# Weights prepared inside the first attention, the gather ahead of the scatter, a mirrored product for the expert lists and a ring of 17 experts

## The chip, the cores and the metric

The kernel runs on one core of one Trainium2 chip. The time is device microseconds (us) of one execution; the kernel before has a median of 3058.5 us over three runs (3056.04 to 3063.08). Less is better.

## What is computed

Two layers, each an attention to a context and a feed-forward part, each added to x behind a gate `tanh(g)`. All data are float32: 4 batches of 512 rows of 512 numbers.

```
x = x + tanh(g_xattn[0]) * L0_xattn(layernorm(x), ctx, mask, wq, bq, wk, bk, wv, bv, wo, bo)   # 16 heads of 32; wq, wo in 8 bits
x = x + tanh(g_ffn[0])   * L0_ffn(layernorm(x), fp4 weights)
x = x + tanh(g_xattn[1]) * L1_xattn(layernorm(x), ctx, ...)                                      # 16 heads of 128, rotary
x = x + tanh(g_ffn[1])   * L1_ffn(layernorm(x), router_w, w_gate, w_up, w_down)

# 8-bit linear: s = max|w| / 127 per row; q = clip(round(w / s)); y = (q_x @ q_w.T) * (s_x * s_w) + b
# L1_ffn: scores = softmax(x @ router_w.T); the 8 best of 64 experts per token, their scores normalised
#         each expert takes its first 128 tokens: y = (silu(x @ w_gate[e]) * (x @ w_up[e])) @ w_down[e]
#         out[token] += y * score
```

## The kernel before

The program runs five stages, one after the other, with a barrier between them: layer0_attention, layer0_ffn, layer1_projections, layer1_attention, layer1_ffn. Each is written per engine, in blocks for SP (which issues the plain DMAs), GpSimd (POOL), ScalarE (ACT), TensorE (PE) and VectorE (DVE). Each engine follows its own list in order; semaphores tie the lists together. The change touches the first and the last stage.

**Start of the first attention.** `layer0_attention` first calls `prepare_layer0_weights` (L713), a stage of its own. There SP loads wq, wo, wk and wv (1 MB each) and five small rows (L733 to L738), and both ScalarE and VectorE wait for all nine. VectorE takes each of wq and wo through a largest value per row (L773), a scale, four scalings (L777), two rounding steps (L778, L779); TensorE transposes the rounded matrices (L758), VectorE copies them to wqT and woT (L790), wo's scales are spread over the partitions by a product with ones (L765) and copied (L794). ScalarE makes the upper halves of wk and wv for products in two parts (L748, L749), VectorE the lower ones (L797). Then come the barrier and the attention: SP loads the first context and x (L315, L318), the context is split in two parts (L415 on ScalarE, L350 on GpSimd), x is normalised and quantised. The first batch's jobs on TensorE follow JOBS_OF_FIRST: four K jobs (each 12 products, L137 to L139 in the helper mm3), four X (transposes of quantised x, L506), S (scales of x), four Q (L515; scaled by VectorE and then by ScalarE, L437), four V. Then scores (L541) of the first four heads, and the loop over groups of four heads: VectorE adds the mask and takes the maximum (shift, L657), ScalarE takes the exponential (L445), TensorE transposes the result (turn, L554), and so on.

**Routing (`route`, L1921).** For four batches of 512 rows, VectorE and TensorE normalise x, multiply it with the router's weights, and write a table of rows (x and the 64 weights of the experts) to HBM. The keys of the chosen tokens are put in keyT, 128 partitions: partition e holds expert e in the first half of the tokens, partition 64 + e the same expert in the second. VectorE takes the 128 largest of each partition by 16 rounds of max and match_replace (L2160, L2161). TensorE then moves the second half's lists to partitions 0 to 63 (L2071); 16 more rounds over both lists (L2168, L2169) give each expert's first 128 tokens; three more steps fill empty slots with the numbers of spare rows, TensorE transposes (L2073), and VectorE writes `slots` (L2177). During routing SP loads the weights of the first 13 experts (L2361, L2362): two at first, then three after each of the four stores of the table; behind them go 17 stores of zeros to second_sum (L1990).

**Experts (`experts`, L2187).** For each of 64 experts: GpSimd gathers 128 rows of the table (L2223), TensorE transposes them (turn_x, L2278), gate and up products (L2288), TensorE transposes h (L2296), down product (L2305), VectorE scales it by the router's weight (L2333), GpSimd scatters it with addition to `out` or, for odd experts, to second_sum (L2232). TensorE's order in iteration e is gate_up(e), turn_h(e - 1), turn_x(e + 1), down(e - 1). Four buffers (AHEAD) hold gathered rows, so that the gather of e + 4 waits for the scaling of e. In GpSimd's list it stands behind the scatter of e. A ring of 13 places (RING_E) holds the experts' weights; SP loads expert e once the down product of e - 13 is done. At the end second_sum is added to `out` by four DMAs (L2239).

Of the kernel before, what the change touches and what calls it, by code (L numbers as in the profile page):

```python
# [178 lines left out]
def make_constants(pool, c, made):  # L179
# [17 lines left out]
JOBS_OF_FIRST = [("K", 0), ("K", 1), ("K", 2), ("K", 3), ("X", 0), ("X", 1), ("X", 2), ("X", 3), ("S", 0),  # L197
                 ("Q", 0), ("Q", 1), ("Q", 2), ("Q", 3), ("V", 0), ("V", 1), ("V", 2), ("V", 3)]
# [45 lines left out]
def layer0_attention(nc, d, x_out):  # L244

    with ExitStack() as ctx:
# [15 lines left out]
        prepare_layer0_weights(nc, d, c, gate, wqT, woT, swq, bqs, bk, swo_row, bv_row, bo_row, wk, wv, bank)  # L262

# [28 lines left out]
        turn_ps, o_ps = bank[4:6], bank[6]  # L292
        names = ("c_loaded c_hi c_lo mhalf_made stat_ready rstd_ready normed x_scaled diagonal x_round x_quant job_done free_act free_dve "
                 "sx_out q_raw q_made scored shifted expd turned ev_act ev_dve weighed oT_out backed o_part o_scaled o_round "
                 "o_quant gbo_made x_biased y_made added step_dve")
# [12 lines left out]
        with nc.Block() as block:  # L308

            @block.sync  # L310
            def _(sp):
                def load(b):
                    if b:
                        sp.wait_ge(s["c_lo"], KC * b)
                    sp.dma_start(ctx_f[:], ctxT_src[b]).then_inc(s["c_loaded"], 16)  # L315
                    if b >= 3:
                        sp.wait_ge(stored[b % 3], 16 * NT)
                    sp.dma_start(x4[:, b % 3], x_src[b]).then_inc(x_loaded[b % 3], 16)  # L318

# [7 lines left out]
                load(0)  # L327
                load_mask(0)
                load_mask(1)
                load(1)  # L330
                for t in range(TILES):
                    sp.wait_ge(s["shifted"], H0 * (t + 1))
                    if t + 2 < TILES:
                        load_mask(t + 2)
                    if t % NT == NT - 1 and t // NT + 2 < B:
                        load(t // NT + 2)
                    if t:
                        store(t - 1)
# [5 lines left out]
            def _(pool):  # L344
                pool.memset(mhalf4[:], -0.5).then_inc(s["mhalf_made"], 1)

# [40 lines left out]
                pool.tensor_scalar(bo_row[:], bo_row[:], gate[:], 1.0, ALU.mult, ALU.mult).then_inc(s["gbo_made"], 1)  # L387
                pool.wait_ge(s["gbo_made"], 1)
                context_lo(0)
                normalise(0)  # L390
                quantise_x(0)
                for G in range(GROUPS0 + DRAIN0):
# [16 lines left out]
            def _(act):  # L409
# [53 lines left out]
                context_hi(0)  # L463
                for job in JOBS_OF_FIRST:
                    evict((job[0], 0, job[1]))
                    make_q((job[0], 0, job[1]))
# [19 lines left out]
            def _(pe):  # L486
                def do(job):
# [5 lines left out]
                    if kind in "KV":  # L493
                        if i == 0:
                            pe.wait_ge(s["c_lo"], KC * b + KC)
                        for a in range(KC):
# [13 lines left out]
                    elif kind == "Q":  # L510
                        if i == 0:
                            by, nth = rank[("X", b, 3)]
                            pe.wait_ge(free[by], nth)
                        for a in range(KC):
# [64 lines left out]

                for job in JOBS_OF_FIRST:  # L580
                    do((job[0], 0, job[1]))
                scores(0)
                for G in range(GROUPS0 + DRAIN0):
# [13 lines left out]
            def _(dve):  # L597
# [92 lines left out]

                dve.wait_ge(s["mhalf_made"], 1)
                statistics(0, 0, NT)
                scale_x(0, 0, NT)
                for job in JOBS_OF_FIRST:
                    evict((job[0], 0, job[1]))
                for G in range(GROUPS0 + DRAIN0):
                    g, b = G % 16, G // 16
                    for i in range(4):
                        shift(4 * G + i)
# [12 lines left out]

def prepare_layer0_weights(nc, d, c, gate, wqT, woT, swq, bqs, bk, swo_row, bv_row, bo_row, wk, wv, bank):  # L713

    with ExitStack() as ctx:
        st = Stage(nc, ctx, "w0")
        sb, sem = st.sb, st.sem
        nat = [sb(f"nat{i}", [P, KC, D], F32) for i in range(2)]
        full = [sb(f"full{i}", [P, KC, D], F32) for i in range(2)]
        q_int = [sb(f"q_int{i}", [P, KC, D], BF16) for i in range(2)]  # L720
        tmp = sb("tmp", [P, KC, D], F32)
        bq = sb("bq", [P, KC], F32)
        amax, scale, inv = (sb(n, [P, 2, KC], F32) for n in ("amax", "scale", "inv"))
        diag = sb("diag", [P, KC, P], F32)
        loaded, made, rounded, turned, copied, spread, spread_out, split_hi, split_lo, step_dve, gated = (
            sem(n) for n in "loaded made rounded turned copied spread spread_out split_hi split_lo step_dve gated".split())
        LOADS = 9
        with nc.Block() as block:

            @block.sync  # L730
            def _(sp):
                for to, of in ((nat[0], "L0_wq"), (nat[1], "L0_wo"), (full[0], "L0_wkT"), (full[1], "L0_wvT")):
                    sp.dma_start(to[:], d[of].rearrange("(k p) n -> p k n", p=P)).then_inc(loaded, 16)  # L733
                sp.dma_start(bq[:], d["L0_bq"].rearrange("(p k) -> p k", p=P)).then_inc(loaded, 16)
                sp.dma_start(bk[:], d["L0_bk"].rearrange("(p k) -> p k", p=P)).then_inc(loaded, 16)
                sp.dma_start(bv_row[:], row_of(d["L0_bv"], 0, D)).then_inc(loaded, 16)
                sp.dma_start(bo_row[:], row_of(d["L0_bo"], 0, D)).then_inc(loaded, 16)
                sp.dma_start(gate[:], row_of(d["g_xattn"], 0, 1)).then_inc(loaded, 16)  # L738

            @block.gpsimd  # L740
            def _(pool):
                make_constants(pool, c, made)

            @block.scalar
            def _(act):
                act.wait_ge(loaded, 16 * LOADS)
                act.activation(gate[:], gate[:], ACT.Tanh).then_inc(gated, 1)
                act.activation(wk[0][:], full[0][:], ACT.Copy).then_inc(split_hi, 1)  # L748
                act.activation(wv[0][:], full[1][:], ACT.Copy).then_inc(split_hi, 1)  # L749

            @block.tensor
            def _(pe):
                pe.wait_ge(made, CONSTS)
                for w in range(2):
                    pe.wait_ge(rounded, w + 1)
                    for j in range(KC):
                        for k in range(KC):
                            mm = pe.transpose(bank[w * KC + j][:, :].bitcast(BF16)[:, k * P:k * P + P],  # L758
                                              q_int[w][:, j, k * P:k * P + P], c["identb"][:])
                        mm.then_inc(turned, 1)  # L760
                pe.wait_ge(spread, 1)

                pe.wait_ge(copied, 1)
                for j in range(KC):
                    mm = pe.matmul(bank[0][:, j * P:j * P + P], c["ones"][:], diag[:, j], start=True, stop=True)  # L765
                mm.then_inc(spread_out, 1)

            @block.vector
            def _(dve):
                step = Chain(dve, step_dve)  # L770
                dve.wait_ge(loaded, 16 * LOADS)
                for w in range(2):
                    step(dve.tensor_reduce(amax[:, w], nat[w][:], AX.X, ALU.max, apply_absolute_value=True))  # L773
                    step(dve.tensor_scalar(scale[:, w], amax[:, w], float(np.float32(1 / 127)), 1e-8, ALU.mult, ALU.max))
                    step(dve.reciprocal(inv[:, w], scale[:, w]))
                    for j in range(KC):
                        step(dve.tensor_scalar(tmp[:, j], nat[w][:, j], inv[:, w, j:j + 1], 127.0, ALU.mult, ALU.min))  # L777
                    step(dve.tensor_scalar(tmp[:], tmp[:], -127.0, ROUND, ALU.max, ALU.add))  # L778
                    dve.tensor_scalar(q_int[w][:], tmp[:], ROUND, None, ALU.subtract).then_inc(rounded, 1)  # L779

                dve.tensor_scalar(swq[:], scale[:, 0], SCALE0, None, ALU.mult)
                dve.tensor_scalar(bqs[:], bq[:], SCALE0, None, ALU.mult)
                dve.wait_ge(made, CONSTS)
                for j in range(KC):
                    ds = dve.tensor_scalar(diag[:, j], c["ident"][:], scale[:, 1, j:j + 1], None, ALU.mult)
                ds.then_inc(spread, 1)
                for w, to in enumerate((wqT, woT)):
                    for j in range(KC):
                        dve.wait_ge(turned, w * KC + j + 1)
                        dve.tensor_copy(to[:, :, j * P:j * P + P],  # L790
# [1389 lines left out]
F1 = 192  # L2180
FP = F1 // 2
AHEAD = 4
RING_E = 13
PARTS = 4


# [245 lines left out]
```

## Time and profile before

| | |
|---|---|
| median of three runs | 3058.5 us |
| the profiled execution | 3060.83 us |
| its span | 3059.0 us |
| TensorE busy | 2639.5 us (86%) |
| VectorE busy | 1738.9 us (57%) |
| ScalarE busy | 1272.6 us (42%) |
| GpSimd busy | 805.6 us (26%) |
| granted TensorE clock, mean | 0.943 |

Times in the rows are from the start of the span. Busy time excludes the issuing of DMAs and waiting. A granted clock of 1.00 is full speed. The first attention runs until about 480 us, the routing from 2498 to 2626 us, the experts from there to 3031 us, and the last addition to the end.

### The profile page before, as it was taken

How to read it: one execution, taken by the hardware profiler on the slowest of the kernel's cores; microseconds unless marked ns; L12 is line 12 of the kernel's file. 1: busy time of each engine (PE TensorE's matmuls, PEld its weight loads, DVE VectorE, ACT ScalarE, POOL GpSimd, SP SyncE). 2: the span in 40 equal slices, each digit the busy share in tenths (PEclk: the TensorE clock that was granted, in tenths of full speed). 3: DMA queues.
4: the chain of work that ended last, by engine and by line, in shares of the span. 5: the costliest groups of instructions: out<-in, count | busy, mean ns of one | idle time of the engine just before them, and what ended most of it. 6: DMA issues, size and time to landing. Idle time of an engine off the chain costs nothing. (4 is left out here: it accounts for less than half of the span.)

```text
span 3059.0 us, 48349 instructions
## 1 busy us (share of the span) xinstructions
PE 2639.5 (86%) x17099; PEld 2107.4 (69%) x17099; DVE 1738.9 (57%) x3888; ACT 1272.6 (42%) x3385; POOL 805.6 (26%) x825
## 2 busy tenths in 40 slices
PE   3888988579999599999699999999999972588885
PEld 2555655479999488887588888888888862345452
DVE  4767676674433566666466666666666647422221
ACT  1666666222222344444355555555555531121111
POOL 2222311000000255555222222222222210244443
PEclk8999998789999799999799999999999986799998
DMA  3010100330000555555712421421331138499986
GB/s 124 12 46 19 46 19 19 111 95 15 29 28 8 173 182 187 192 186 186 222 50 56 134 54 43 124 67 40 91 109 42 36 102 291 127 290 290 272 219 113
DMA packets 227055, 340.10 MB, mean 111 GB/s; under 512 B 24512, under 2 KB 110976, under 8 KB 226304
## 3 DMA queue, kind: packets, MB, share of 16 engines
q1 hardware_dynamic: 211904, 297.14, 31.3%
q0 software_dynamic: 14912, 39.85, 5.8%
q8 instruction: 139, 2.28, 0.3%
q14 instruction: 100, 0.82, 0.1%
HBM read 230.60 MB, written 110.53 MB: 112 GB/s over the span
## 5 line engine op out<-in xcount | busy, mean ns | idle before, releaser
L1706 POOL TENSOR_SCALAR a_prob<-a_prob,a_rinv 128x640 f32<-128x640 f32 (+3 forms) x256 | 252.4, 986 | 770.2 <-DVE a_rinv L1861 770.2
L1851 DVE TENSOR_REDUCE a_mx<-a_s_ps 128x1 f32<-128x640 f32 (+3 forms) x256 | 262.3, 1025 | 274.2 <-PE a_s_ps L1775 267.9
L1727 ACT ACTIVATE a_probT<-a_t_ps 128x512 fp32r<-128x512 f32 (+3 forms) x512 | 237.2, 515 | 369.4 <-PE a_t_ps L1783 369.4
L1867 DVE TENSOR_TENSOR a_probT<-a_t_ps,a_probT 128x512 fp32r<-128x512 f32 (+3 forms) x512 | 276.7, 582 | 47.2 <-ACT a_probT L1727 47.1
L1718 ACT ACTIVATE a_prob<-a_s_ps,a_nb,a_rs 128x640 f32<-128x640 f32 (+3 forms) x256 | 267.7, 1046 | 0.0
L137 PE MATMUL a_o_ps<-a_probT,a_v 128*128 128x256 f32 x832 | 245.4, 295 | 0.0
L139 PE MATMUL a_o_ps<-a_probT,a_v 128*128 128x256 f32 x832 | 235.1, 283 | 0.0
L138 PE MATMUL a_o_ps<-a_probT,a_v 128*128 128x256 f32 x832 | 235.1, 283 | 0.0
L1783 PE MATMUL a_t_ps<-a_ident,a_prob 128*128 128x128 f32 x1664 | 225.9, 274 | 8.5 <-DVE a_probT L1867 5.9
L137 PE MATMUL f_bank<-f_xT,f_gu 128*128 128x256 f32 x704 | 204.9, 291 | 19.1 <-DVE f_gu L1114 19.1
L554 PE MATMUL a_bank<-a_ident,a_prob 128*128 128x128 f32 x1024 | 168.2, 291 | 58.9 <-ACT a_prob L445 33.8
L554 PEld LDWEIGHTS a_bank<-a_ident,a_prob 128*128 128x128 f32 x1024 | 113.4, 144 | 152.7 <-ACT a_prob L445 112.8
L1783 PEld LDWEIGHTS a_t_ps<-a_ident,a_prob 128*128 128x128 f32 x1664 | 194.4, 141 | 31.3 <-issue 6.1
L138 PE MATMUL f_bank<-f_xT,f_gu 128*128 128x256 f32 x704 | 203.6, 289 | 0.0
L139 PE MATMUL f_bank<-f_xT,f_gu 128*128 128x256 f32 x704 | 203.5, 289 | 0.0
L445 ACT ACTIVATE a_prob<-a_prob,a_nmax 128x512 f32<-128x512 f32 x256 | 182.1, 716 | 18.6 <-DVE a_nmax L657 18.6
L2325 DVE SCALAR_TENSOR_TENSOR e_h<-e_th,e_gu_ps 128x192 f32<-128x192 f32 x64 | 22.7, 355 | 282.1 <-ACT e_th L2266 282.1
L2288 PE MATMUL e_gu_ps<-m_wgu,e_xT 128*128 128x384 f32 x512 | 180.0, 495 | 1.4 <-ACT e_xT L2249 1.4
L137 PE MATMUL p_bank<-p_w,p_xT 128*128 128x512 f32 x384 | 159.6, 416 | 17.0 <-DVE p_w L1475 11.8
L657 DVE CUSTOM_DVE_ANT_0 a_prob<-a_bank,a_mask 128x512 f32<-128x512 f32 x256 | 161.5, 687 | 18.4 <-PE a_bank L541 13.4
L138 PEld LDWEIGHTS a_o_ps<-a_probT,a_v 128*128 128x128 f32 x832 | 158.5, 190 | 5.6
L137 PEld LDWEIGHTS a_o_ps<-a_probT,a_v 128*128 128x128 f32 x832 | 158.3, 190 | 5.5
(299 smaller groups left out, 6737.9 us busy)
## 6 DMA issues: line engine op xcount, KB each, us to landing
m_wgu<-in_w_gate SPq DMA_DIRECT2D x64, 384.0 KB, 3.9
m_wgu<-in_w_up SPq DMA_DIRECT2D x64, 384.0 KB, 5.4
m_wd<-in_w_down SPq DMA_DIRECT2D x64, 384.0 KB, 7.6
l_q_hi<-p_turned SPq DMA_DIRECT2D x64, 256.0 KB, 2.7
l_q_lo<-p_turned SPq DMA_DIRECT2D x64, 256.0 KB, 2.5
a_qT<-l_q_hi SPq DMA_DIRECT2D x64, 256.0 KB, 3.6
a_qT<-l_q_lo SPq DMA_DIRECT2D x64, 256.0 KB, 4.2
l_v_hi<-p_vs SPq DMA_DIRECT2D x32, 256.0 KB, 2.7
```

Of the source, the lines that this page charges most:

```text
L137: pe.matmul(out, ll, rh, start=first, stop=False, **kw)
L138: pe.matmul(out, lh, rl, start=False, stop=False, **kw)
L139: return pe.matmul(out, lh, rh, start=False, stop=last, **kw)
L445: act.activation(prob[:, n % RING0], prob[:, n % RING0], ACT.Exp, bias=nmax[:, n % RING0:n % RING0 + 1], scale=-1.0, accum_out=rsum[:, T % ...
L554: mm = pe.transpose(turn_ps[n % 2][:, a * P:a * P + P], prob[:, n % RING0, a * P:a * P + P], c["ident"][:])
L1706: pool.tensor_scalar(prob[:, k % 4, 0:w], prob[:, k % 4, 0:w], rinv[:, k % 4:k % 4 + 1], 1.0, ALU.mult, ALU.mult).then_inc(s["weighted"], 1)
L1718: act.activation(prob[:, k % 4, 0:w], s_ps[:, k % 2, 0:w], ACT.Exp, bias=nb[:, k % 4:k % 4 + 1], scale=rs[:, u, h:h + 1], accum_out=rsum[: ...
L1727: act.activation(probT[0][:, pair % 2, i * 4:i * 4 + n, k % 2], t_ps[i][:, 0:n * P].rearrange("p (m n) -> p m n", n=P), ACT.Copy).then_inc ...
L1783: mm = pe.transpose(t_ps[i][:, m * P:m * P + P], prob[:, k % 4, (i * 4 + m) * P:(i * 4 + m + 1) * P], c["ident"][:])
L1851: step(dve.tensor_reduce(mx[:, k % 4:k % 4 + 1], s_ps[:, k % 2, 0:w], AX.X, ALU.max))
L1867: dve.tensor_tensor(probT[1][:, pair % 2, i * 4:i * 4 + n, k % 2], t_ps[i][:, 0:n * P].rearrange("p (m n) -> p m n", n=P), probT[0][:, pai ...
L2288: mm = pe.matmul(gu_ps[e % 2][:, 0:2 * F1], xT[:, e % 2, k], wgu[:, u, :, k], start=(k == 0), stop=(k == KC - 1))
```

## The change

1. `prepare_layer0_weights` is gone. The same steps are put into the lists of `layer0_attention`, in buffers that its first batch does not use yet. SP loads the context first, then wk, x, wv, wq, wo. The V jobs move ahead of the X jobs. VectorE quantises wq before the V evictions and finishes wo after the first four shifts; TensorE waits for wo before its first turn.
2. The second 16 rounds of the lists are gone. The list of 128 partitions is transposed at once; a product with a mirrored identity turns the second half's list upside down, so that it fills the first half's empty slots from the back. Four VectorE steps write `slots`. The last match_replace of the first rounds is left out.
3. The ring has 17 places. Routing's x, table and transposed x lie in the last six of them; their loads (experts 11 to 16) go behind the stores of zeros and a wait for the table's stores.
4. In the experts, GpSimd issues the gather of e + 4 before the scatter of e.

The core of the diff:

```diff
-JOBS_OF_FIRST = [("K", 0), ("K", 1), ("K", 2), ("K", 3), ("X", 0), ("X", 1), ("X", 2), ("X", 3), ("S", 0),
-                 ("Q", 0), ("Q", 1), ("Q", 2), ("Q", 3), ("V", 0), ("V", 1), ("V", 2), ("V", 3)]
+JOBS_OF_FIRST = [("K", 0), ("K", 1), ("K", 2), ("K", 3), ("V", 0), ("V", 1), ("V", 2), ("V", 3),
+                 ("X", 0), ("X", 1), ("X", 2), ("X", 3), ("S", 0), ("Q", 0), ("Q", 1), ("Q", 2), ("Q", 3)]
...
@@ SP
+                load_context(0)
+                sp.dma_start(k_full, rows(d["L0_wkT"])).then_inc(s["wk_loaded"], 16)
+                sp.dma_start(bk[:], columns("L0_bk")).then_inc(s["wk_loaded"], 16)
+                load_x(0)
+                sp.dma_start(v_full, rows(d["L0_wvT"])).then_inc(s["wv_loaded"], 16)
...
+                sp.dma_start(natural[0], rows(d["L0_wq"])).then_inc(s["wq_loaded"], 16)
...
+                sp.dma_start(natural[1], rows(d["L0_wo"])).then_inc(s["wo_loaded"], 16)
...
@@ ACT
                 context_hi(0)
+                act.wait_ge(s["wk_loaded"], 32)
+                act.activation(wk[0][:], k_full, ACT.Copy).then_inc(s["kw_hi"], 1)
+                act.wait_ge(s["wv_loaded"], 32)
+                act.activation(wv[0][:], v_full, ACT.Copy).then_inc(s["vw_hi"], 1)
...
@@ PE
+                pe.wait_ge(s["consts_made"], CONSTS)
                 for job in JOBS_OF_FIRST:
+                    if job == ("X", 0):
+                        turn_weights(0)
                     do((job[0], 0, job[1]))
                 scores(0)
+                turn_weights(1)
+                spread_scales()
+                pe.wait_ge(s["w_copied"], 2 * KC + 1)
@@ DVE
+                dve.wait_ge(s["kw_hi"], 1)
+                dve.tensor_tensor(wk[1][:], k_full, wk[0][:].bitcast(F32), ALU.subtract).then_inc(s["kw_lo"], 1)
                 dve.wait_ge(s["mhalf_made"], 1)
                 statistics(0, 0, NT)
+                dve.wait_ge(s["vw_hi"], 1)
+                dve.tensor_tensor(wv[1][:], v_full, wv[0][:].bitcast(F32), ALU.subtract).then_inc(s["vw_lo"], 1)
                 scale_x(0, 0, NT)
-                for job in JOBS_OF_FIRST:
+                dve.wait_ge(s["wq_loaded"], 32)
+                largest(0)
+                step(dve.tensor_scalar(swq[:], wscale[:, 0], SCALE0, None, ALU.mult))
+                step(dve.tensor_scalar(bqs[:], bq[:], SCALE0, None, ALU.mult))
+                scale_weights(0)
+                round_weights(0)
+                for i in range(2):
+                    evict(("V", 0, i))
+                dve.wait_ge(s["wo_loaded"], 48)
+                largest(1)
+                for i in range(2, 4):
+                    evict(("V", 0, i))
+                copy_weights(0, wqT)
+                scale_weights(1)
+                for job in JOBS_OF_FIRST[8:]:
                     evict((job[0], 0, job[1]))
+                for i in range(4):
+                    shift(i)
+                round_weights(1)
...
+                ds.then_inc(s["spread"], 1)
+                copy_weights(1, woT)
+                dve.wait_ge(s["spread_out"], 1)
+                dve.tensor_copy(swo_row[:], bank[4][:]).then_inc(s["w_copied"], 1)
...
@@ route
                 for j in range(B):
                     store_tab(j)
-                    prefetch(2 + 3 * j, min(5 + 3 * j, RING_E))
+                    prefetch(2 + 3 * j, min(5 + 3 * j, RING_E - SHARED_E))
                 for g in range(OUT_ROWS // P):
                     sp.dma_start(second[g * P:g * P + P], zeros[:, 0:D]).then_inc(s["zero_stored"], 16)
+                sp.wait_ge(s["logits_done"], B * NT)
                 for u in range(2):
                     sp.wait_ge(stored[u], 16 * (B // 2))
+                prefetch(RING_E - SHARED_E, RING_E)
...
-                pe.matmul(slot_ps[0:E, 0:CAP], c["ident"][:, E:2 * E], lists[:, 0], start=True, stop=True).then_inc(s["moved"], 1)
-                pe.wait_ge(s["firsts_ready"], 1)
-                pe.transpose(slot_ps[:, CAP:CAP + E], first[:], c["ident"][0:E, 0:E]).then_inc(s["slots_turned"], 1)
+                pe.transpose(slot_ps[:, 0:P], lists[:], c["ident"][:]).then_inc(s["lists_turned"], 1)
+                pe.wait_ge(s["turned_copied"], 1)
+                pe.matmul(slot_ps[:, P:P + E], mirror[:], turned[:, 1], start=True, stop=True).then_inc(s["mirrored"], 1)
...
-                both = lists[0:E].rearrange("e l n -> e (l n)")
-                for r in range(CAP // TOP):
-                    best8 = first[:, r * TOP:r * TOP + TOP]
-                    step(dve.max(best8, both))
-                    step(dve.match_replace(both, best8, both, 0.0))
...
+                step(dve.scalar_tensor_tensor(chosen[:], turned[:, 0], 0.0, slot_ps[:, P:P + E], ALU.is_equal, ALU.mult))
+                step(dve.tensor_tensor(chosen[:], chosen[:], turned[:, 0], ALU.add))
+                step(dve.tensor_scalar(spare[:], chosen[:], 0.0, slot_no[:], ALU.is_equal, ALU.mult))
+                dve.scalar_tensor_tensor(slots[:, 0:E], spare[:], float(T), chosen[:], ALU.add, ALU.subtract).then_inc(s["slots_ready"], 1)
...
@@ experts
                     pool.wait_ge(s["scaled"], e + 1)
+                    gather(e + AHEAD)
                     if e >= 2:
                         pool.wait_ge(scattered[e % 2], 16 * (e // 2))
                     pool.indirect_dma_start((out, second)[e % 2][:], bass.IndirectOffsetOnAxis(ap=slots[:, e:e + 1], axis=0), yw[:, e % AHEAD], None,
                                             bounds_check=OUT_ROWS - 1, compute_op=ALU.add).then_inc(scattered[e % 2], 16)
-                    gather(e + AHEAD)
...
-RING_E = 13
+RING_E = 17
+SHARED_E = 6
```

## Rows read from the trace of the kernel before

**Rows 1.** Timeline, first 55 us: start us, us, engine, line, what.

```profile
16.16 2.29 DVE L773 TENSOR_REDUCE w_amax<-w_nat 128x4 f32<-128x2048 f32 x1 [16.16 <-DMA a_gate<-in_g_xattn]
...
29.47 1.23 DVE L779 TENSOR_SCALAR w_q_int<-w_tmp 128x2048 bf16<-128x2048 f32 x1
...
32.44 2.02 PE L765 MATMUL a_bank<-w_diag,a_ones 128*128 128x128 f32 x8
32.86 1.42 DVE L790 COPY a_woT<-a_bank 128x512 bf16<-128x512 bf16 x4
...
35.10 2.28 DVE L797 TENSOR_TENSOR a_wk<-w_full,a_wk 128x2048 fp32r<-128x2048 f32 x1
...
40.26 0.38 SPq L315 DMA_DIRECT2D a_ctx_f<-in_ctxT  x1
...
51.49 0.80 PE L137 MATMUL a_bank<-a_ctx_s,a_wk 128*128 128x512 f32 x1 [17.03 <-POOL a_ctx_s L350]
```

**Rows 2.** DMA issues, 0 to 80 us: count, KB, us to landing (issue at 2.33).

```profile
w_full<-in_L_wvT SPq DMA_DIRECT2D x1, 1024.0 KB, 11.8
```

**Rows 3.** Timeline, 64 to 87 us.

```profile
64.38 1.33 PE L506 MATMUL a_bank<-a_identb,a_qx 128*128 128x128 bf16 x16
...
69.20 3.50 ACT L437 ACTIVATE a_q<-a_qraw,a_bqs,a_swq 128x512 f32<-128x512 f32 x4 [1.99 <-DVEq L638]
...
70.62 0.58 PE L137 MATMUL a_bank<-a_wv,a_ctx_s 128*128 128x512 f32 x1
...
82.77 1.14 PE L541 MATMUL a_bank<-a_k,a_q 32*128 32x512 f32 x8 [0.88 <-DVE a_v L640]
...
85.62 1.37 PE L554 MATMUL a_bank<-a_ident,a_prob 128*128 128x128 f32 x8 [1.72 <-ACT a_prob L445]
...
85.86 0.69 DVE L657 CUSTOM_DVE_ANT_0 a_prob<-a_bank,a_mask 128x512 f32<-128x512 f32 x1
```

**Rows 4.** Timeline, end of the routing.

```profile
2606.27 1.21 DVE L2161 MATCH_REPLACE8 r_keyT<-r_lists,r_keyT 128x1024 f32<-128x1024 f32 x1
2607.59 0.69 PE L2071 MATMUL r_slot_ps<-r_lists,r_ident 128*64 128x128 f32 x2 [42.24 <-DVEq L2162]
...
2625.67 0.22 DVE L2177 CAST m_slots<-r_slot_ps 128x64 uint32<-128x64 f32 x1 [0.46 <-PE r_slot_ps L2073]
```

**Rows 5.** Timeline of SP in the routing: the stores of zeros.

```profile
2574.53 15.43 SPq L1990 DMA_DIRECT2D second_sum<-r_zeros  x17
```

**Rows 6.** Chain of waits in the experts: start us, us, what.

```profile
2709.09 0.75 PE e_x_ps L2278 x4
2709.84 1.73 PE e_y_ps L2305 x4
...
2711.59 0.76 DVE e_yw L2333
...
2713.15 1.25 POOL second_sum L2232
...
2715.04 6.30 DMA e_xg<-token_table,m_slots
...
2794.23 2.90 PE e_y_ps L2305 x4
```

**Rows 7.** The scalings as one group, 2646 to 2958; chain, last experts.

```profile
L2333 DVE TENSOR_SCALAR e_yw<-e_y_ps,e_xg x51: 749/751/752, 2646.3 to 2953.9; 128x512 f32<-128x512 f32 x51
...
3000.53 2.58 PE e_gu_ps L2288 x8
3005.78 2.58 PE e_gu_ps L2288 x8
```

**Rows 8.** Stretches: us, busy PE, PEld, DVE, ACT, POOL, PEclk, DMA share, GB/s.

```profile
2788.00:2798.00 10.00, 7.75 (x23) 4.33 (x22) 2.21 (x4) 1.20 (x3) 2.64 (x2) 0.83 0.80 230
2646.30:2957.40 311.10, 273.99 (x910) 155.99 (x909) 73.71 (x151) 60.25 (x151) 133.79 (x102) 0.97 0.98 281
```

**Rows 9.** Timeline of TensorE within 2788 to 2798.

```profile
2793.10 1.13 PE L2278 MATMUL e_x_ps<-e_ident,e_xg 128*128 128x128 f32 x4 [2.25 <-DMA e_xg<-token_table,m_slots]
```

More of the change, by code:

```diff
@@ L311, in _, with load_context @@
             def _(sp):
-                def load(b):
+                def load_context(b):
                     if b:
@@ L335, in _ @@
                     if t % NT == NT - 1 and t // NT + 2 < B:
-                        load(t // NT + 2)
+                        load_context(t // NT + 2)
+                        load_x(t // NT + 2)
                     if t:
@@ L689, in scale_out, with largest, scale_weights @@
                         dve.reciprocal(oinv[:, u:u + 1], os[:, u:u + 1]).then_inc(s["o_scaled"], 1)
+                def largest(w):
+                    step(dve.tensor_reduce(wmax[:, w], natural[w], AX.X, ALU.max, apply_absolute_value=True))
+                    step(dve.tensor_scalar(wscale[:, w], wmax[:, w], float(np.float32(1 / 127)), 1e-8, ALU.mult, ALU.max))
+                    step(dve.reciprocal(winv[:, w], wscale[:, w]))
+                def scale_weights(w):
+                    for j in range(KC):
+                        step(dve.tensor_scalar(scaled_w[:, j], natural[w][:, j], winv[:, w, j:j + 1], 127.0, ALU.mult, ALU.min))
@@ new lines, in round_weights, with copy_weights @@
+                def round_weights(w):
+                    step(dve.tensor_scalar(scaled_w, scaled_w, -127.0, ROUND, ALU.max, ALU.add))
+                    if w:
+                        dve.wait_ge(s["w_turned"], KC)
+                    dve.tensor_scalar(q_int, scaled_w, ROUND, None, ALU.subtract).then_inc(s["w_rounded"], 1)
+                    dve.wait_ge(s["w_rounded"], w + 1)
+                def copy_weights(w, to):
+                    for j in range(KC):
+                        dve.wait_ge(s["w_turned"], w * KC + j + 1)
+                        dve.tensor_copy(to[:, :, j * P:j * P + P],
+                                        bank[4 + j][:, :].bitcast(BF16)[:, 0:D].rearrange("p (k n) -> p k n", k=KC)
+                                        ).then_inc(s["w_copied"], 1)
@@ L696, in _ @@
+                dve.wait_ge(s["spread_out"], 1)
+                dve.tensor_copy(swo_row[:], bank[4][:]).then_inc(s["w_copied"], 1)
+                dve.wait_ge(s["gated"], 1)
                 for G in range(GROUPS0 + DRAIN0):
                     g, b = G % 16, G // 16
-                    for i in range(4):
+                    for i in range(4 if G else 0):
                         shift(4 * G + i)
@@ L709, in _ @@
                             scale_x(b + 1, 2 * (g - 3), 2 * (g - 3) + 2)
-        st.clear()
[L713 to L790, printed above, removed]
-                                        bank[w * KC + j][:, :].bitcast(BF16)[:, 0:D].rearrange("p (k n) -> p k n", k=KC)
-                                        ).then_inc(copied, 1)
-                dve.wait_ge(spread_out, 1)
-                dve.tensor_copy(swo_row[:], bank[0][:])
-                for i, w in enumerate((wk, wv)):
-                    dve.wait_ge(split_hi, i + 1)
-                    dve.tensor_tensor(w[1][:], full[i][:], w[0][:].bitcast(F32), ALU.subtract).then_inc(split_lo, 1)
@@ L1918, with route @@
 HALF = T // 2
-def route(nc, d, x_in, table, out, slots, load, second):
+def route(nc, d, x_in, table, out, slots, ring, load, second):
     with ExitStack() as ctx:
@@ L1946, in route @@
         keyT = sb("keyT", [P, HALF], F32)
-        lists = sb("lists", [P, 2, CAP], F32)
-        first = sb("first", [E, CAP], F32)
-        empty = keyT[0:E, 0:CAP]
+        lists = sb("lists", [P, CAP], F32)
+        turned = sb("turned", [P, 2, E], F32)
+        chosen, spare = sb("chosen", [P, E], F32), sb("spare", [P, E], F32)
         x_ps = [ps(f"x_ps{i}", [P, D], F32) for i in range(NT)]
@@ L2362, in load @@
             eng.dma_start(wd[:, u], d_src[e]).then_inc(w_loaded[u], 16)
-        route(nc, d, x_in, table, out, slots, load, second)
+        route(nc, d, x_in, table, out, slots, ring, load, second)
         experts(nc, table, out, second, slots, wgu, wd, w_loaded, load)
```

102 lines of the change are left out of this document (76 added, 26 removed).

## Prediction

> **What bounds the kernel now.** I read the busy slices first, then the stretches that the change touches (the start, the routing, the experts) instruction by instruction, then the chain of waits. At the start VectorE sets the pace: it prepares the weights from 16.2 us on, and only when all is ready does the attention ask for its context (40.26) and start its first product (51.49); the first attention weights are turned at 85.62 [rows 1, 3]. Between the two attentions nothing is edited. In the routing VectorE alone makes the lists: a last round ends at 2607.5, the merging of two lists per expert ends with the slot numbers at 2625.9 [rows 4]. In the experts TensorE is busy for 274 of 311 us, and the DMA engines 0.98 of the time [rows 8]. Two readings of that stretch are possible. The chain of waits repeats this loop, two experts long: the gather lands, its rows are turned (0.75), the down product of two experts before (1.73) ends, VectorE scales it (0.76), GpSimd issues the scatter (1.56 from the scale's start), and the next gather only 1.89 later; that one lands 6.30 after its start [rows 6]. The sum is 0.75 + 1.75 + 1.56 + 1.89 + 6.30 + 0.05 = 12.3 us for two experts, 6.15 each, and the count agrees: 51 scalings, the first at 2646.3, the last at 2953.9, are 50 steps of 6.15 us [rows 7]. The other reading is that the transfers fill the DMA engines. 311.1 us at 281 GB/s are 87.4 MB, 1.72 MB per expert; that the rate stays at 281 could be the cause of the 6.15 or its result. Without loads TensorE goes on at 5.25 us per expert (3000.53 to 3005.78) [rows 7].
>
> **Part 1, weights prepared inside the attention.** The old chain to 40.26 goes; its pieces come back beside the first products. Landing: the fourth megabyte landed at 2.33 + 11.8 = 14.1 us [rows 2], about 2.65 us each after a first at some 6.2, so context 6.2, wk 8.9, x 11.5, wv 14.5, wq 17.2, wo 20 with its small rows 21.5. The context's split took until 11.2 us after its issue (40.26 to 51.49), so it is ready at 12.0. ScalarE's copy of wk (taken as long as VectorE's subtraction of it, 2.28) ends at 11.2, the subtraction at 13.5: products begin at 13.6. K takes 12.9 (51.49 to 64.38), to 26.5; V, now next, about 11.1 (from 70.62 to some 1.0 before 82.77), to 37.6 [rows 1, 3]. In that time VectorE does statistics and scaling of x and quantises wq; the old chain needed (30.7 - 16.16)/2 = 7.3 us per matrix [rows 1], x some 9 from its landing (an estimate: eight steps of about 0.7 [rows 3] and GpSimd's between them), so wq is ready near 30.5 and V's products hide it (7 us to spare). On the path again: 16 transposes of wq and their copies, 1.9 us (an estimate: the copies alone are 1.42), to 39.5; then X, S and Q to the last q, 8.3 (64.38 to 72.70), to 47.8; scores and four shifts, 3.8 (82.77 to 86.55), to 51.6 [rows 1, 3]. Then wo: two rounding steps of 1.23, to 54.1; the diagonal (estimated at 0.9) beside the transposes, copies 1.42, to 56.4; the scales spread 2.0 and copied 0.7 (as long as a shift), to 59.1 [rows 1, 3]. TensorE waits for all this before turn(0), which now stands at 85.62: **26.5 us less**. Bounds: ScalarE, VectorE and GpSimd wait in new places (ScalarE's wv copy is ahead of its K evictions; VectorE's V evictions stand behind the quantising of wq and the largest of wo). If wo's last steps (7.5 us) hid wholly behind other work the gain would be 34; if wq's quantising ended 7 us later than I have it and then some, 20. I take 26.5, as both were followed step by step.
>
> **Part 2, lists.** From the end of the last round to the slot numbers are now 2625.89 - 2607.48 = 18.4 us [rows 4]. The last match (1.21 + 0.09) goes too. New: a turn of 128x128 on TensorE (two half products took 0.69, with 0.1 ahead), a copy (0.3), the mirrored product (0.4 to 0.7), four steps on 128x64, nearest to the final cast's 0.22, with 0.05 between: 0.8 + 0.3 + 0.6 + 1.1 = 2.8, say 3.0; ends 2 and 4.5. That makes 1.3 + 18.4 - 3.0 = **16.7 us**. VectorE was the only engine at work there, so all of it counts, if SP is done by then.
>
> **Part 3, the ring.** Loads 11 to 16 are issued behind the 17 zero stores and a wait for the tables. SP needed 15.43 us for those 17, 0.91 each [rows 5]: it is held by the filled queue. Starting between 2569 (six load issues of before are out of the way) and 2574.5, with 18 issues at 0.91 to 1.36 (by size, 384 to 256 KB), SP ends between 2601 and 2614; slots are ready at 2609.2. So cost 0 to 5, taken 0. In the experts four loads fewer remain (47 for 51), 4.7 MB. With gathers as the bound that is worth nothing.
>
> **Part 4, gather ahead of scatter.** The 1.89 us leave the loop: 12.3 - 1.9 = 10.4 us for two experts, 5.2 each, and TensorE's own 5.25 takes over. The gather no longer has its expert's scatter just ahead in GpSimd's queue. The scatter comes 1.4 us later; behind it on GpSimd is only the next wait for a scaling, and it has two experts (10.5 us) to land. With no slack, gathers that land late still cost: I put 0.15 us per expert, 5.40: 50 x (6.15 - 5.40) = **38 us** (ends: 5.25 gives 45; 5.96, see A, 12). The clock is part of this: after TensorE had waited 2.25 us for a gather, its four transposes took 1.13 for 0.75 and the down product after them 2.90 for 1.73, 1.6 us more, and the granted clock of 2788 to 2798 is 0.83 where the whole stretch has 0.97: for a part of these 10 us it was at the lower of its levels, 1.2 GHz [rows 6, 8, 9].
>
> A row first: gathers took 6.30 us while loads kept the DMA engines at 0.98 [rows 6, 8]. The Trainium skill (DMA: Bandwidth & Descriptors, "Queues, rings and completion order") says that each DMA engine takes turns between its queues, a packet at a time. By that rule a longer line of loads in SP's queue would not lengthen a gather in GpSimd's, and the experts would reach 5.25, 45 us; no run here shows it under a longer line.
>
> **Sum.** 26.5 + 16.7 + 38 = 81.2. The profiled span is 3059.0 us, its time 3060.8 (1.8 outside the span), 2.3 above the median of the three runs, 3058.5. 3060.8 - 81.2 - 2.3 = 2977.3: **2977 us**.
>
> **Rivals.** (A) The DMA engines are the bound. For it: share 0.98 [rows 8]. With the missing 0.02 used, and 1% more, 1.72 MB need 5.96 us. Against: the chain runs through gathers, never through a load [rows 6], and a line of loads can grow by 0.7 us per expert for 47 experts, 33 us, before it uses up the ring's 17 x 5.25 = 89. It holds only if gathers are stretched with the loads. Then 46 steps of 5.96 and four of 5.25 take 295 us for 307.6: 26.5 + 16.7 + 12.4 = 55.6, **3003 us**. (B) The start and SP's late loads cost more: wq not hidden (20 for 26.5) and SP 3.5 us late, together 10: **2987 us**. (C) Slower: behind the longer line of loads gathers land so late that TensorE idles 2.2 us and the clock falls each time. One turn of two experts is then 10.5 + 2.2 + 1.6 = 14.3, 7.15 each, which loses 50 us against the 43 of parts 1 and 2. That begins at gathers of 10.5 + 2.2 - 4.1 = 8.6 us, where 6.30 is the row; against it speaks that the DMA engines are full already while it takes 6.30. At 9.5 us a turn is 15.2, 7.6 each, and the time 3058.5 - 43.2 + 72.5 = **3088 us**. (D) The new order does not do what it says: the gather, started 1.9 us earlier, takes 1.9 us longer, as it now competes with more of the loads. Then only parts 1 and 2 stay, **3015 us**.
>
> **How the numbers follow.** Forecast (5.25 to 5.6 us per expert) 0.62; A 0.18; B 0.10; D 0.07; C 0.03. The forecast's own range is 2962 to 2992 (experts -7 and +10, start -8 and +7, not all at once). The range for 8 in 10 takes A and B in and leaves C, most of D and a double gain out: **2957 to 3010**. About 0.2%, 6 us, is what can be told from no change. All but C are faster by more; C starts about at no change: faster 0.97, within 0.01, slower 0.02.
>
> **What would show it.** In the changed kernel: first K product near 13.6 and first transposed attention weights near 59 us; slot numbers some 3 us after the last maximum; SP's last ring load issued before them; gather issue 0.8 us after each scaling's end, scatter behind it; TensorE's idle time before the transposes of gathered rows down to a quarter; steps of scaling 5.25 to 5.5. The forecast falls if gathers take over 6.7 us from issue to landing, if TensorE begins to wait for ring loads, or if the first turn stands beyond 65 us.

## The result and the profile after

The changed kernel takes 3009.2 us (median of four runs, 3002.4 to 3010.7) against 3057.3 before: a ratio of 0.984, 95% interval 0.982 to 0.986, 48 us less where 81 were forecast. The kernel before has a median of 3057.3 us here, and of 3062.0 and 3060.3 beside the two sets of experiments below; kernels of different sets can be compared to some 5 us only. The profiled execution has a span of 3006.6 us for 3059.0, and these 52.4 us can be placed by where each stage begins in the two traces:

| stretch | before | after | less | forecast |
|---|---|---|---|---|
| start of the span to the first DMA of the routing | 2498.1 | 2471.7 | 26.4 | 26.5 |
| routing, to the first gather | 130.4 | 117.4 | 13.0 | 16.7 |
| first gather to last scatter | 397.3 | 384.4 | 13.0 | 38 |
| last scatter to the end | 33.2 | 33.2 | 0 | 0 |

So the experts gave 25 us less than forecast and the routing 4. The start first, in the timeline of the changed kernel (start us, us, engine, line, what):

```profile
14.23 0.77 PE L137 MATMUL a_bank<-a_ctx_s,a_wk 128*128 128x512 f32 x1 [14.23 <-DVE a_wk L777]
...
49.38 2.09 PE L580 MATMUL a_bank<-a_k,a_q 32*128 32x512 f32 x8 [3.74 <-ACT a_q L465]
...
56.60 1.89 PE L625 MATMUL a_bank<-a_identb,a_probT 128*128 128x128 bf16 x16 [5.13 <-DVE a_probT L766]
...
59.10 2.04 PE L633 MATMUL a_bank<-a_diag,a_ones 128*128 128x128 f32 x8 [0.61 <-DVE a_woT L772]
61.18 0.69 DVE L808 COPY a_swo_row<-a_bank 128x512 f32<-128x512 f32 x1 [2.23 <-PE a_bank L633]
61.93 1.97 PE L593 MATMUL a_bank<-a_ident,a_prob 128*128 128x128 f32 x8 [0.79 <-DVE a_swo_row L808]
```

The first product stands at 14.2 where it stood at 51.49 [rows 1], and turn(0) at 61.93 where it stood at 85.62 [rows 3]. That is 23.7 us, and it is what the edit gives where it ends. The other 2.7 do not come from it. Followed through the two traces, the lead falls to 19.7 us by 473 us of the kernel before (copies of L666, now L728) and rises to 26.8 by the end of the first attention, which lasts until 564 us and not 480. The same instructions took 74.0 us before and 66.9 after there, beside another granted clock (us, busy PE, PEld, DVE, ACT, POOL, granted clock, DMA share, GB/s; first before, then after):

```profile
473.00:547.00 74.00, 61.19 (x647) 37.12 (x647) 52.02 (x148) 46.91 (x124) 11.45 (x12) 0.88 0.05 16
```

```profile
453.30:520.20 66.90, 53.96 (x645) 33.58 (x647) 51.90 (x148) 46.85 (x124) 11.48 (x12) 1.00 0.05 17
```

Seven kernels here have the new start. In their traces turn(0) stands at 61.0 to 62.0 us, but the routing begins anywhere from 2466.1 to 2473.7, where the three kernels with the old start have 2495.8 to 2498.4. So 22 to 32 us of lead reach the routing, though the edit gives nearly the same each time.

The lists in the routing, same view:

```profile
2582.50 1.23 DVE L2196 MAX8 r_lists<-r_keyT 128x8 f32<-128x1024 f32 x1
...
2583.93 0.45 PE L2107 MATMUL r_slot_ps<-r_ident,r_lists 128*128 128x128 f32 x1 [41.02 <-DVEq L2199]
2584.42 0.29 DVE L2202 COPY r_turned<-r_slot_ps 128x128 f32<-128x128 f32 x1 [0.45 <-PE r_slot_ps L2107]
...
2584.77 0.69 PE L2109 MATMUL r_slot_ps<-r_turned,r_mirror 128*128 128x64 f32 x2 [0.38 <-DVE r_turned L2202]
...
2586.37 0.23 DVE L2209 SCALAR_TENSOR_TENSOR m_slots<-r_spare,r_chosen 128x64 uint32<-128x64 f32 x1
```

From the last maximum (2583.73) to the slots (2586.60) are 2.9 us, where 18.4 followed the last replacement of before [rows 4].

In the experts the chain of waits still runs through the gather (start us, us, what):

```profile
2702.74 1.73 PE e_y_ps L2339 x4
...
2704.49 0.76 DVE e_yw L2367
...
2706.02 7.68 DMA e_xg<-token_table,m_slots
...
2713.74 0.75 PE e_x_ps L2312 x4
2714.49 1.73 PE e_y_ps L2339 x4
...
2717.77 8.12 DMA e_xg<-token_table,m_slots
```

The scatter is gone from the loop: the gather starts 1.53 us after the scaling's start and not 3.45 [rows 6]. But it takes 7.7 to 8.1 us and not 6.3. A turn of two experts is 0.75 + 1.75 + 1.53 + 7.7 = 11.7 to 12.2 us for 12.3. GpSimd's rows show the two steps of a turn: 5.25, then mostly 6.2 to 7.3. TensorE is busy for 175 us of the 200 from 2660 to 2860, for 177 in the kernel before. From the second to the 51st scatter the mean step is 5.95 for 6.17, in the last twelve before the last it is 5.14 for 5.64.

### The profile page after: what moved, and what is told of

The parts are those of the page before. It is cut to its first block and busy times, and to the rows that moved or that the text cites. A ratio compares the mean times of both kernels' runs of the same rounds, so it can differ in the third digit from the quotient of the medians.

```text
span 3006.6 us, 48204 instructions
## 1 busy us (share of the span) xinstructions
PE 2631.6 (88%) x17077; PEld 2105.2 (70%) x17099; DVE 1724.5 (57%) x3837; ACT 1274.4 (42%) x3385; POOL 809.0 (27%) x827
## 5 line engine op out<-in xcount | busy, mean ns | idle before, releaser
L2322 PE MATMUL e_gu_ps<-m_ring,e_xT 128*128 128x384 f32 x512 | 179.2, 493 | 1.4 <-ACT e_xT L2283 1.4
L719 DVE CUSTOM_DVE_ANT_0 a_prob<-a_bank,a_mask 128x512 f32<-128x512 f32 x256 | 161.4, 687 | 19.3 <-PE a_bank L580 14.3
L1416 ACT ACTIVATE p_sq<-p_bank 128x128 f32<-128x128 f32 x384 | 101.1, 278 | 146.6 <-PE p_bank L139 146.6
L138 PEld LDWEIGHTS a_o_ps<-a_probT,a_v 128*128 128x128 f32 x832 | 158.4, 190 | 5.6
```

The costliest lines, as they stand in the source:

```text
L138: pe.matmul(out, lh, rl, start=False, stop=False, **kw)
L2322: mm = pe.matmul(gu_ps[e % 2][:, 0:2 * F1], xT[:, e % 2, k], wgu[:, u, :, k], start=(k == 0), stop=(k == KC - 1))
```

## The experiments

Two theories for the step of 5.95. Theory 1 is rival A: the transfers fill the DMA engines, and bytes by rate set the step. Theory 2: the loop through the gather sets it, and the gather has become longer. The first four kernels were to tell them apart, and to find out what the ring and the lists do by themselves.

### The old order in the changed kernel

```diff
                     pool.wait_ge(s["scaled"], e + 1)
-                    gather(e + AHEAD)
...
                     pool.indirect_dma_start((out, second)[e % 2][:], ...)
+                    gather(e + AHEAD)
```

> The changed kernel with the old order on GpSimd: scatter of e, then gather of e + 4. Theory 1 (the DMA engines are full with 285 GB/s and set the step of about 5.95 us per expert, whichever goes first): gathers take 6.3 us again instead of 7.8, the step stays within 0.05 us of 5.95, the whole within 3 us of the changed kernel's 3009. Theory 2 (the loop through the gather sets the step and the gather was stretched only because its place moved): the loop gets its 1.9 us back and the gather stays near 7.8, step 6.15 or more, 10 us or more slower than 3009.

Measured: 3018.6 us, 0.987 of before (0.984 to 0.990) where the changed kernel has 0.984 (0.982 to 0.986); by the traces the stretch from first gather to last scatter is 390.6 us for 384.4. The medians of the two sets, 3018.6 and 3009.2, differ by 9.4 us, or by 4.7 when each is taken from the kernel before run beside it, and the intervals of the ratios overlap. Over all the traces with four buffers and all loads, that stretch is 390.1 to 397.3 us with the scatter first (four kernels, the kernel before and two with its expert code among them) and 380.5 and 384.4 with the gather first. So the order is worth something between 6 and 17 us. The step is 6.03 for 5.95, just outside what theory 1 allowed and below the 6.15 of theory 2. The gather's length settles part of it. The view by tile of the gathered rows, 2660 to 2860 us, gives GpSimd's issues and the time to landing (first this kernel, then the changed one):

```profile
L2257 POOL DMA_INDIRECT e_xg<-token_table,m_slots x33: 1052/1056/1058, 2661.0 to 2855.4; - x33
DMA to landing us min/median/max: 5.0/6.1/7.1
```

```profile
L2257 POOL DMA_INDIRECT e_xg<-token_table,m_slots x33: 1054/1055/1057, 2664.1 to 2855.3; - x33
DMA to landing us min/median/max: 6.8/7.6/8.4
```

With the scatter first a gather takes 6.1 us, with the gather first 7.6. Of the 1.9 us by which it starts earlier, 1.5 are lost on its way. Each theory got one thing wrong here: the gather did go back to 6.1, and the order did bring something.

### Six buffers of gathered rows

```diff
+ROWS_AHEAD = 6
-RING_E = 17
+RING_E = 16
-        xg = sb("xg", [P, AHEAD, ROW], F32)
+        xg = sb("xg", [P, ROWS_AHEAD, ROW], F32)
-                    gather(e + AHEAD)
+                    gather(e + ROWS_AHEAD)
```

> The changed kernel with six buffers of gathered rows instead of four (the gather of e + 6 behind the scaling of e), ring of 16 to make room. Theory 1 (transfers as a whole set the step): TensorE no longer waits for its own expert's gather at first, but the step stays near 5.95 while loads run, total 3009 +- 4. Theory 2 (latency of the gather through a loop of two experts sets the step, loads may lag behind in a ring of 16): the step falls to 5.25 to 5.3, loads land later and later, the experts lose 25 to 30 us, total 2980 to 2985.

Measured: 2972.5 us (2971.2 to 2975.6), 0.971 of before (0.969 to 0.973), 37 us less than the changed kernel. The step is 5.25 from the second expert to the 51st, TensorE's own. Theory 1 falls for the step of 5.95: the bytes per expert are the same and the step is faster. The gathers are no shorter, and the loads now land late. DMA issues of this kernel, 2720 to 2780 us (count, KB, us to landing):

```profile
m_ring<-in_w_down SPq DMA_DIRECT2D x10, 384.0 KB, 26.1
e_xg<-token_table,m_slots POOLq DMA_INDIRECT x12, 7.6
out_rows<-e_yw,m_slots POOLq DMA_INDIRECT x6, 8.9
```

And the view by tile of its gathered rows, 2660 to 2860 us:

```profile
DMA to landing us min/median/max: 7.1/7.6/8.9
```

A load lands 26 us after its issue, five experts later, and late in the stage SP also issues it late: the w_down of expert 60 is issued at 2867.7 and lands at 2892.7, that of expert 28 landed at 2690.3. That is one expert's loads per 6.3 us, while TensorE goes on at 5.25. The ring's head start pays for the difference: expert 28 has its weights 54 us before its first product (2743.9), expert 60 has them 19 us before (2912.1). The gather takes 7.6 us, as in the changed kernel, where loads land after 9.5. A line of loads that takes 16 us longer to land does not lengthen it. The Trainium skill (DMA: Bandwidth & Descriptors, "Queues, rings and completion order") says that a DMA engine takes turns between its queues packet by packet, and this agrees: the length of the other queue's line does not count, only that there is one.

### A ring of 13

```diff
-RING_E = 17
+RING_E = 13
```

> The changed kernel with a ring of 13 instead of 17 (the last six places still share routing's rows; seven experts loaded early, six late). The first transpose of gathered rows stood 6.7 us after the first gather's start in the changed kernel, 3.9 in the kernel before. If four more loads still in flight cause that, the ring of 13 gives 3.9 again (3 us back), and its four loads more in the experts cost 4 x 0.7 = 3 us where transfers set the step (theory 1), nothing where the gather loop does (theory 2): total 3009 by theory 1, 3006 by theory 2.

Measured: 3002.3 us, 0.980 of before (0.978 to 0.983), lower than the changed kernel by some 7 us where 0 or 3 were expected. The first gather and its transposes, changed kernel and this one (timeline; rows between them left out):

```profile
2589.07 1.34 POOL L2257 DMA_INDIRECT e_xg<-token_table,m_slots  x1 [0.59 <-issue]
...
2595.81 1.10 PE L2312 MATMUL e_x_ps<-e_ident,e_xg 128*128 128x128 f32 x4 [10.36 <-DMA e_xg<-token_table,m_slots]
```

```profile
2584.88 1.34 POOL L2257 DMA_INDIRECT e_xg<-token_table,m_slots  x1 [0.59 <-issue]
...
2588.81 1.10 PE L2312 MATMUL e_x_ps<-e_ident,e_xg 128*128 128x128 f32 x4 [7.54 <-DMA e_xg<-token_table,m_slots]
```

6.7 us in the changed kernel, 3.9 here: the loads of the last places are still in flight when the first gather starts, as expected. The last of the changed kernel, issued at 2575.8, took 19.3 us and landed at 2595.1; with the ring of 13 the DMA engines stand idle in the 5 us before the first gather. With a ring of 16 (six buffers) it is 4.1 us, so the delay comes with the 17th place. With four loads more in the experts the step did not rise (5.90 for 5.95). Another 3.5 us are in the routing; the next kernels show that this is not the ring. The larger ring brings nothing at a step that the gather sets, and costs the 2.8.

### The new lists alone

```diff
 the kernel before, with the list steps, the mirror and their order
 of the changed kernel; ring of 13, x, tab and xT in buffers of their own
```

> The kernel before with the new lists alone (one transpose, mirrored product, four steps, no last replace), ring of 13 and everything else as before. The changed kernel's trace has 2.9 us from the last maximum to the slots for 18.4, a gain of 16.8 there, but the routing as a whole shrank by 13.0 only. If the missing 3.9 is the clock of TensorE in routing (a chance of how its idle times fall) or the shared ring, this run gives 16.8 off 3057: 3040; if the lists themselves cause it, 3044.

Measured: 3040.0 us (3034.5 to 3047.4), 0.993 of before (0.9905 to 0.995): 17 us under the 3057.3 of the first comparison, 22 under the kernel before run beside it (3062.0). The times agree with the 16.8 of the trace but do not exclude 13. The trace has 2.9 us from the last maximum to the slots here too. The profiled execution (span 3045.0) lies near the upper end of the times, and its routing lost 3.7 us again: the first maximum of the lists stands 71.8 us after the routing's first DMA, 68.1 in the kernel before. So the routing as a whole gives 13.2 of the 14.0 us between the two spans, without the shared ring, which is thereby not the cause. The loss stands 50 to 60 us after the routing's first DMA, beside a lower granted clock (kernel before, then this one; columns as above):

```profile
2548.10:2558.10 10.00, 7.95 (x48) 7.81 (x48) 4.19 (x11) 4.06 (x15) 0.00 (x0) 0.70 1.05 323
```

```profile
2548.40:2558.40 10.00, 7.81 (x37) 7.81 (x38) 3.11 (x7) 3.57 (x12) 0.49 (x1) 0.50 1.02 320
```

Four more kernels tested what was left: why the gather is longer, whether the deep buffers need the new order or a ring over 13, what the first attention gives alone, and where the 4 us of the routing come from.

### No loads of w_up

```diff
-                    pe.wait_ge(w_loaded[u], 48 * (e // RING_E + 1))
+                    pe.wait_ge(w_loaded[u], 48 + 32 * (e // RING_E))
...
-            for i in range(2):
+            for i in range(2 if e < RING_E else 1):
                 eng.dma_start(wgu[:, u, i], gu_src[i][e]).then_inc(w_loaded[u], 16)
```

> The changed kernel without the loads of w_up for experts 17 to 63: the weights of the place's expert before are used, so the output of those experts is another one. Theory 2a (a gather is stretched by the loads that it runs beside: 7.6 us whenever a line of loads is there, 5.0 without): with 0.79 MB for 1.18 per expert and four buffers the line is gone for part of the gather, it takes 5.5 to 6.5 us and the step is 5.25 to 5.3, TensorE's own. Theory 2b (the gather is stretched by its place alone, ahead of the scatter): it stays at 7.5 and the step at 5.95.

Measured: 2972.4 us (two runs, 2971.2 and 2973.5), 0.972 of before (0.969 to 0.974), step 5.25 with four buffers. The gather, same view and stretch:

```profile
DMA to landing us min/median/max: 3.5/6.0/6.5
```

With a third of the load bytes gone and the gather still ahead of the scatter it takes 6.0 us. So it is the loads beside it that stretch it, theory 2a; 2b falls. At 6.0 the loop needs (0.75 + 1.75 + 1.53 + 6.0) / 2 = 5.0 us, under TensorE's 5.25, and does not show.

### Six buffers with a ring of 13

```diff
 as the kernel with six buffers, and
-RING_E = 16
+RING_E = 13
```

> The changed kernel with six buffers of gathered rows and a ring of 13. Loads took 21 to 25 us to land with the ring of 16 and six buffers; a ring of 13 gives them some 60 us. So the step stays at 5.25 if theory 2 holds, and the first gather, with fewer late loads beside it, is transposed 3 us earlier: total 2969 +- 4 against 2972 with the ring of 16. If the ring of 13 runs short (theory 1 in a late form), TensorE waits for loads near the end and the total is 2980 or more.

Measured: 2972.2 us (2966.9 to 2973.9), 0.971 (0.969 to 0.973), as with the ring of 16. Step 5.25; first scatter 20.2 us after the first gather, also as with 16 (23.2 with 17). The ring of 13 is enough here, but only just. The DMA share falls from 0.97 (2910 to 2920 us) to 0.49 (2920 to 2925) when the last loads are through, and the last expert's first product starts at 2928.8. What the transfers reach, changed kernel, then this one (us, busy PE, PEld, DVE, ACT, POOL, granted clock, DMA share, GB/s):

```profile
2660.00:2860.00 200.00, 175.26 (x601) 100.88 (x602) 48.11 (x99) 40.67 (x102) 88.83 (x67) 1.00 1.05 291
```

```profile
2660.00:2860.00 200.00, 200.00 (x686) 115.55 (x685) 55.73 (x116) 45.54 (x114) 100.83 (x77) 1.00 1.06 299
```

The DMA share is full in both, 1.05 and 1.06, and yet TensorE is busy for 175 us in one and all 200 in the other. A full share did not mean that the transfers set the step; the bytes in this stretch are only 3% more at a step 12% shorter, since the loads are the part that waits.

### Six buffers in the kernel before

```diff
 the kernel before, with
+ROWS_AHEAD = 6
-        xg = sb("xg", [P, AHEAD, ROW], F32)
+        xg = sb("xg", [P, ROWS_AHEAD, ROW], F32)
-                    gather(e + AHEAD)
+                    gather(e + ROWS_AHEAD)
```

> The kernel before with six buffers of gathered rows alone: scatter still ahead of gather, ring of 13. Theory 2: the loop through the gather spans three or more experts, so the order of the two does not matter any more, the step falls from 6.17 to 5.25 and the total by some 50 us, to 3010. Length of the gather: if a permanent line of loads sets it, it rises from 6.1 to some 7.6 although the order is the old one; if the order sets it, it stays at 6.1. Theory 1: step near 6.0, total 3050.

Measured: 3016.1 us (3012.7 to 3020.1), 0.986 of before (0.984 to 0.988), 44 us less, by two buffers alone. The step is 5.29 with the old order, for 5.25 with the new one: what the order brings with four buffers is nearly gone with six. The stretch from first gather to last scatter is 350.9 us for 347.3, and most of the 3.6 stands near the end, where TensorE waits before its gate and up products, 2.0 us the longest:

```profile
2955.19 2.82 PE L2289 MATMUL e_gu_ps<-m_wgu,e_xT 128*128 128x384 f32 x8 [2.02 <-issue]
```

The profile names no releaser, but of the three things that these products wait for, the transposed rows and the buffer of h were ready; what is left is the weights (w_down of this expert was issued at 2930.2, with the DMA share at 1.06). Here the ring of 13 ran short.

The gather's length, which this run was also to show, is not in its trace, because nobody waits for a gather any more; that part stays open. Its routing gives the 4 us away:

```profile
2515.80:2525.80 10.00, 10.00 (x58) 10.00 (x58) 2.51 (x6) 2.84 (x9) 1.01 (x1) 0.60 0.62 184
```

This is the stretch from 20 to 30 us after the routing's first DMA, same columns. The granted clock is 0.60, so most of it is at 1.2 GHz, and the first maximum of the lists comes 72.0 us after the first DMA. The routing here is that of before, line for line, where it was 68.1.

### The first attention alone

```diff
 the changed kernel up to layer1_attention;
 route, experts and layer1_ffn of the kernel before
```

> The kernel before with the new first attention alone. From the trace of the changed kernel the routing starts 26.4 us earlier; nothing between is changed, so this gives 3057 - 26 = 3031 +- 4. If part of those 26 us came from elsewhere (a clock that falls otherwise), it is 3036 or more.

Measured: 3026.1 us (3022.0 to 3030.2), 0.990 of before (0.988 to 0.9915), 34 us less than the kernel before run beside it (3060.3), 31 less than the first comparison's 3057.3; more than the 26 expected, and just outside the 3027 to 3035 that I gave. The start itself is no better than in the changed kernel (turn(0) at 61.3 us); the routing begins 32.0 us earlier than before, and the stretch from first gather to last scatter, with the code of before, took 390.1 us for 397.3. Its routing is also that of before, and its clock in the same stretch is high:

```profile
2486.10:2496.10 10.00, 7.17 (x65) 7.03 (x64) 6.41 (x27) 3.24 (x12) 0.29 (x1) 0.92 0.66 177
```

The first maximum stands at 67.8 us. So the same routing code has run in 67.8 and in 72.0 us.

## Why the prediction was right or wrong

**The start: right in its steps, 2.8 us too high, and its sum met by luck.** K's first product was expected at 13.6 and stands at 14.2; VectorE's subtraction of wk took 3.05 for 2.28. X starts at 39.4, as forecast (39.5). X, S and Q then took 10.0 us for 8.3, and 0.9 more were lost at the scores and shifts, where TensorE was granted 0.50 of its clock (scores 2.09 us for 1.14). The first turn came at 61.9 for 59.1, which makes 23.7 us and not 26.5. That 26.4 had been gained when the routing began is drift in stages that nobody edited: 19.7 at 473 us, 26.8 at the end of the first attention, and 22 to 32 at the routing in the seven kernels with this start. I had no term for it.

**The lists: right.** 2.9 us for 3.0, and 16.8 for 16.7 in this stretch. In the routing as a whole 13.0 remained, beside a clock of TensorE that rose later: in the changed kernel's trace the stretch from 20 to 30 us after the routing's first DMA has 0.59, where before has 0.94. It is not the change: the kernel before with six buffers, which has the old routing, shows 0.60 and 72.0 us, and the one with the first attention alone 0.92 and 67.8. The kernel with the lists alone had 0.98 there and lost its 3.7 us later, where it was granted 0.50 for 0.70. I had no term for it. No run changed the clock alone, and what decides when it rises is open.

**The ring: right that it brings nothing, wrong that it costs nothing.** SP was done in time (105.5 us after the first DMA, slots at 114.9), as forecast. But my bounds looked only at SP. The transfers that it had issued were still under way and held up the first gather by 2.8 us. The kernel with a ring of 13 shows it. The loads saved in the experts were worth nothing there, as forecast.

**The order of gather and scatter: the term that failed.** I priced it at 38 us; the experts gave 13.0 in all, and by the runs with either order it is worth 6 to 17. The step of the working was "the 1.89 us leave the loop: 12.3 - 1.9 = 10.4": it kept the gather's 6.30 us as a constant. That row was measured for a gather that starts 3.4 us after the loads of the same turn are issued, when part of them is through. Started 1.9 us sooner it meets more of them, and takes 7.6 us. Rival D said just this, at 1.9 us longer; it was 1.3 to 1.5, and I gave D 0.07. A longer line of loads would have done no harm (7.6 us with either line); it was the gather's start that moved. The forecast's own sign of failure, gathers over 6.7 us, came true.

**Rival A had the right number and the wrong reason.** Its step of 5.96 was met (5.95), and its time of 3003 is 6 us off, as is D's 3015 on the other side. But the DMA engines do not set the step of 5.95: with two more buffers it is 5.25 at the same bytes per expert. The argument that I had against A, that loads may lag behind in the ring, was sound for these 64 experts (26 us to land, no wait). The line grew faster than the 0.7 us per expert that I had: 6.3 less 5.25, about 1.1. With a ring of 13 it was nearly used up in one kernel and ran short in another. So the transfers are the next bound, and more experts would meet it. It lacked one thing: with four buffers there is no slack for a gather of 7.6 us. By my own loop the change needed one of 6.4.

**The range** of 2957 to 3010 held 3009 by 1 us, and only by the weight given to A, whose cause was not the one at work; 2977 itself was 32 us off. That it held is luck. B did not occur as such. C needed gathers of 8.6 us; the longest in 2660 to 2860 was 8.4.

## What to carry to other kernels

The time to landing of a DMA is no constant that stays when its start is moved: when a transfer is put earlier, ask what else is in flight at the new moment, and price it by a row in which it had that company. Where a loop is bound by latency and the DMA engines show a full share, one more buffer is the better lever than a shorter chain: two buffers of 2.3 KB per partition gave 44 us in the old kernel, and the new order 6 to 17. That lasts as long as the loads are ahead. A full DMA share says that the engines have work, not that anybody waits for it; look at which transfer the chain of waits goes through, and which ones can lag, and for how long. And before a gain of a few us is put down to an edit, follow it through the trace from where the edit ends: here the lead moved between 19.7 and 26.8 us in code that both kernels share.

## What the runs showed of the hardware

- A gather of 128 rows of 2304 bytes took 6.1 us when it started behind its scatter, 7.6 ahead of it, 6.0 ahead of it with a third of the load bytes gone, and 7.6 with loads landing 26 us late. It was longer by the loads that it ran beside, not by the length of their line.
- The same routing instructions took 67.8 or 72.0 us to the first maximum, where TensorE's granted clock averaged 0.92 or 0.60 some 20 us in. The same instructions near the end of the first attention took 66.9 or 74.0 us at 1.00 or 0.88. That is spread that belongs to no edit, and as much as several of the edits here were meant to bring.
- With TensorE at 5.25 us per expert, one expert's 1.18 MB of loads landed every 6.3 us beside the gathers and scatters, at a DMA share of 1.06.
- The fastest kernels here, 2972 us, are the changed one with six buffers of gathered rows, with a ring of 16 or of 13.
